# Moving the sum of squares of a gated norm from GpSimd alone to ScalarE and GpSimd, and reordering the work at a group's end

## The chip, the cores and the metric

One core of one Trainium2 chip runs the whole program. The metric is device time in microseconds (us) for one execution, the median of several runs. The engines are TensorE (PE in the profile, its weight loads PEld), VectorE (DVE), ScalarE (ACT), GpSimd (POOL) and SyncE (SP), which issues the DMAs. Each engine runs its own queue in order; the queues are tied together by semaphores alone.

## The reference, cut to what matters

The program is a chain of four blocks over 1024 tokens of 512 features (4 sequences of 256), each followed by `x = layernorm(x + block(x))`: A (a Taylor-like attention and a feed-forward), B (a feed-forward with LoRA), C (a Mamba2-like state space block) and D (a ternary feed-forward). The change touches C alone. Of it:

```
u      = x @ in_proj.T                 -> gate (8192), xs (8192), B, C (8 groups x 128), dt (128)
xs     = silu(causal_conv4(xs)),  B, C likewise
Y      = chunked scan(xs, dt, B, C) + xs * D                 (128 heads of 64)
y      = Y * silu(gate)
y      = y * rsqrt(mean of y*y over each group of 1024 + eps) * norm_w      (8 groups)
out    = y @ out_proj.T                                      (8192 -> 512)
```

The mean of squares runs over the 1024 features of a group, so the factor of a group is known only when all of the group's features are.

## The kernel before, in words

Stage C works on 64 units of 128 features (two heads of 64). Eight units make a group. Features stand on the partitions and the 1024 tokens along the free axis, in halves of 512, each in a PSUM bank. `Unit(g, p, j)` is unit `U = 8g + 2p + j`: group g, pair p (0 to 3), member j. `V = U - 1` is the unit before it. `for_units` writes the two bodies of pair 0 out and loops over pairs 1 to 3; group 0 is written out and groups 1 to 7 are a loop. After it comes a unit called `last`, which only finishes.

The units are software-pipelined by hand. The body of unit U does, on each engine, in this order:

* TensorE: input projection of x for U (`in_x`, 12 matmuls of 512 columns for each half), the scan's matmuls for V (`inside`), two small ones that make exponents (`seg`, L1712 and L1713), the gate's projection (`in_g`, 24 matmuls), four token tiles of the output projection of the pair before (`out_tile`, 6 matmuls each), and transposes (`turn`, L1746). All wide products are three fp32r products of split operands, a high part and a low part.
* VectorE: the last low part of y (`y_low`, L1210), the convolution (six L1124), `y_inside` (L1198) and `y_gated` (L1205) of V, `clamp` (eight L1242), and then the decay products (`decay_round`, six L1230, which count `m_done`) mixed with four `out_add` (L1221, which adds an output bank to `group_out`) and two `x_steps` (L1250).
* ScalarE: taps, the high part of the next x weights (L1468), SiLUs, exponentials (with two loads of its function table a unit, ahead of L1553 and L1539), the high part of the next gate weights (`gate_weights`, L1472), and high parts of y (`y_high`, L1505).
* GpSimd: the low parts of the weights (`low`, L1365, for x and for the gate; `out_low`, L1373) and the squares: `squares` waits until VectorE has done all six decay products of U, squares y of V (L1386) and adds the squares to `sq_sum` (L1389). For the first unit of a group L1384 writes the squares to `sq_sum` directly.

The order in GpSimd's body is: `out_low` (if j is 0), low part of the x weights, squares, low part of the gate weights, `out_low` (if j is 1), and the group's sums where a group has ended. TensorE's `in_g` waits for the gate's low part (`g_w_lo`), and `out_tile` of a j = 0 unit for `out_w_lo`.

A group's outputs are summed unscaled in `group_out` and scaled at the end. The last unit of a group is finished in the body of (g, 0, 0) of the next. In the body of (g, 0, 1) TensorE, after the first half of `in_x`, waits for the sum of squares and adds it over the partitions (`squares_sum`, 8 fp32 products with a vector of ones, L1757), VectorE takes the mean (`mean_square`), ScalarE the root, VectorE the reciprocal and the scaled addition of tiles 0 to 3 to x (`group_add`, L1271). ScalarE scales tiles 4 to 7 (`group_scaled`, L1572), GpSimd adds them to x (`group_sum`, L1396) and then clears the whole of `group_out` (L1399), all at the end of the same body. The next thing in GpSimd's queue is `out_low` of unit (g, 1, 0).

Of the kernel before, what the change touches and what calls it, by code (L numbers as in the profile page):

```python
# [10 lines left out]
ALU = mybir.AluOpType  # L11
# [5 lines left out]
P = 128  # L17
# [24 lines left out]
GROUPS = 8  # L42
# [860 lines left out]
class Unit:  # L903


    def __init__(self, g, p, j):
        self.g, self.p, self.j = g, p, j
        self.U = g * UPG + p * 2 + j
        self.V = self.U - 1
        self.first_pair = isinstance(g, int) and g == 0 and isinstance(p, int) and p == 0  # L910
        self.first = self.first_pair and j == 0
        self.group_first = isinstance(p, int) and p == 0 and j == 0
        self.after_group_first = isinstance(p, int) and p == 0 and j == 1
        self.group_ends = self.group_first and not self.first
        self.group_ended = self.after_group_first and not self.first_pair


def for_units(eng, body):

    def group(g):  # L920
        for j in range(2):
            body(Unit(g, 0, j))
        with eng.Fori(1, PAIRS) as p:
            for j in range(2):
                body(Unit(g, p, j))
    group(0)
    with eng.Fori(1, GROUPS) as g:
        group(g)


def state_space(nc, sh, dram):
# [3 lines left out]
    with Stage(nc) as ctx:  # L935
        def sb(name, shape, dt=F32):
            return ctx.enter_context(nc.sbuf_tensor(f"C_{name}", shape, dt))

        def sem(name):
# [34 lines left out]
        first_count = sb("first_count", [P, 2])  # L974
# [17 lines left out]
            group_zero""".split()  # L992
# [136 lines left out]
        def _(v):  # L1129
# [84 lines left out]
            def out_add(u, k):  # L1214

                t = 4 * u.j + k
                v.wait_ge(S.out_mm, (u.U - 2) * 4 + (k + 1))
                if k == 0:
                    v.wait_ge(S.out_added, (u.U - 2) * 4 + OUT0)
                    v.wait_ge(S.group_zero, u.g if u.group_first or u.after_group_first else u.g + 1)  # L1220
                v.tensor_tensor(group_out[:, t, :], bank[OUT_BANK[k % 4]][:, :], group_out[:, t, :], ALU.add)\  # L1221
                 .then_inc(S.out_added, 1)
# [38 lines left out]
            def group_scale(g):  # L1261
                v.wait_ge(S.std_done, g)
                v.wait_ge(S.group_done, (g - 1) * TT + ONE0)
                v.reciprocal(rstd[:, :], ms[:, :]).then_inc(S.rstd_done, 1)
# [17 lines left out]
            v.memset(first_count[:, 1:2], 0.0).then_inc(S.sq_added, ONE0)  # L1282
            v.wait_ge(S.consts_in, 32)
# [72 lines left out]
            for hf in range(2):  # L1356
                group_add(GROUPS, range(HT * hf, HT * (hf + 1)), (last.U - 2) * 4 + TT)
                v.wait_ge(S.group_done, (GROUPS - 1) * TT + HT * (hf + 1) + ONE0)
                norm.vector(v, hf)

        @block.gpsimd
        def _(e):
# [13 lines left out]
            def squares(u):  # L1376

                y, sq = xs[:, 1 - u.j, :], sg[:, 1 - u.j, :]
                e.wait_ge(S.gated, u.V * 2 + 2)
                if u is not last:  # L1380
                    e.wait_ge(S.m_done, u.U * ROUNDS + ROUNDS)
                if u.after_group_first:
                    wait(e, S.ms_mm, u.g)
                    e.tensor_tensor(sq_sum[:, :], y, y, ALU.mult).then_inc(S.squared, 1)  # L1384
                else:
                    e.tensor_tensor(sq, y, y, ALU.mult).then_inc(S.squared, 1)  # L1386
                    e.wait_ge(S.squared, u.U)
                    e.wait_ge(S.sq_added, added_before(u) + ONE0)
                    e.tensor_tensor(sq_sum[:, :], sq_sum[:, :], sq, ALU.add).then_inc(S.sq_added, 1)  # L1389

            def group_sum(u, g):

                for i in range(HT):
                    t = HT + i
                    e.wait_ge(S.group_scaled, (g - 1) * HT + (i + 1))
                    e.tensor_tensor(sh.x[:, t, :], group_out[:, t, :], sh.x[:, t, :], ALU.add).then_inc(S.group_done, 1)  # L1396
                e.wait_ge(S.group_zero, 1)
                e.wait_ge(S.group_done, g * TT + ONE0)
                e.memset(group_out[:, :, :], 0.0).then_inc(S.group_zero, 1)  # L1399
# [9 lines left out]
            e.wait_ge(S.dt_moved, 5)  # L1409
            e.wait_ge(S.dt_chain_v, DT_V)  # L1410
            e.memset(group_out[:, :, :], 0.0).then_inc(S.group_zero, 1)

            def body(u):
# [16 lines left out]
        def _(a):  # L1430
# [136 lines left out]

            def group_scaled(u, g):
                a.wait_ge(S.rstd_done, g + ONE0)
                a.wait_ge(S.out_added, (u.U - 1) * 4 + OUT0)  # L1570
# [4 lines left out]
            def body(u):  # L1575
# [25 lines left out]
            y_high(last, 0)  # L1601
            y_high(last, 1)
# [293 lines left out]
```

## Time and profile before

| what | value |
|---|---|
| median of 3 runs | 2421.09 us (2419.13 to 2422.48) |
| the profiled execution's own time | 2417.13 us |
| its span, first to last instruction | 2415.4 us |
| mean granted TensorE clock | 0.946 of full |
| TensorE busy in the span | 2165.9 us (90%) |
| VectorE, ScalarE, GpSimd busy | 1803.1, 1156.4, 826.7 us |

The span is the sum of four stages that run one after the other. Stage C begins at about 510 us, its units at about 650 us, and they end at about 2166 us. The share of an engine over the span says little about a stage: what matters is how long one unit takes, and what TensorE waits for in it.

### The profile page before, as it was taken

The numbers are of one execution on the slowest core, as the hardware profiler recorded it, in microseconds if no ns is written. First come the engines' busy times: TensorE is split into PE (matmuls) and PEld (weight loads), VectorE is DVE, ScalarE is ACT, GpSimd is POOL, SyncE is SP. The second block draws the span as 40 slices with busy tenths as digits, with TensorE's granted clock in tenths as the row PEclk, the third lists the DMA queues.
The fourth block names the chain that finished last, engine by engine and source line by source line (L and its number), as shares of the span: only waits on it lengthen the run. The fifth ranks groups of instructions, "written<-read, shape, count | busy, mean of one in ns | idle before, by whom it ended". The sixth has DMA issues, their size and how long they took to land. (4 is left out here: it accounts for less than half of the span.)

```text
span 2415.4 us, 36570 instructions
## 1 busy us (share of the span) xinstructions
PE 2165.9 (90%) x10769; PEld 1720.9 (71%) x10833; DVE 1803.1 (75%) x2969; ACT 1156.4 (48%) x2118; POOL 826.7 (34%) x478
## 2 busy tenths in 40 slices
PE   7999499979899989989989989989989989975987
PEld 6777387867777767767767777777777767754865
DVE  6444446449778878979878878878878878977887
ACT  2112114333366656655656656656656656631222
POOL 5434133411123434434344334425334443430000
PEclk9999699989999989989999999999999999987998
DMA  4211412322222212211221222211121221202433
GB/s 149 92 40 57 143 64 79 104 41 103 72 96 66 79 45 66 79 44 58 65 66 44 66 62 60 66 57 60 49 79 44 66 79 44 70 1 93 143 116 106
DMA packets 125941, 175.68 MB, mean 73 GB/s; under 512 B 17668, under 2 KB 83716, under 8 KB 125316
## 3 DMA queue, kind: packets, MB, share of 16 engines
q1 hardware_dynamic: 125892, 175.07, 22.8%
q8 instruction: 26, 0.43, 0.1%
q14 instruction: 23, 0.19, 0.0%
HBM read 165.72 MB, written 9.31 MB: 72 GB/s over the span
## 5 line engine op out<-in xcount | busy, mean ns | idle before, releaser
L70 PE MATMUL bank<-xT_hi,C_w_hi 128*128 128x512 f32 x1160 | 480.9, 415 | 32.1 <-POOL C_w_lo L1365 25.3
L71 PE MATMUL bank<-xT_lo,C_w_hi 128*128 128x512 f32 x1160 | 465.4, 401 | 0.0
L72 PE MATMUL bank<-xT_hi,C_w_lo 128*128 128x512 f32 x1160 | 465.3, 401 | 0.0
L1386 POOL TENSOR_TENSOR C_sg<-C_xs 128x1024 f32<-128x1024 f32 x56 | 130.8, 2336 | 677.3 <-DVE C_decay L1230 677.3
L1124 DVE SCALAR_TENSOR_TENSOR C_acc<-bank,C_par,C_acc 128x510 f32<-128x510 f32 (+2 forms) x384 | 285.8, 746 | 85.5 <-ACT C_acc L1432 56.3
L70 PEld LDWEIGHTS bank<-xT_hi,C_w_hi 128*128 128x128 f32 x1160 | 223.4, 193 | 97.8 <-POOL C_w_lo L1365 41.0
L72 PEld LDWEIGHTS bank<-xT_hi,C_w_lo 128*128 128x128 f32 x1160 | 222.4, 192 | 54.7
L1221 DVE TENSOR_TENSOR C_group_out<-bank,C_group_out 128x512 f32<-128x512 f32 x256 | 175.1, 687 | 112.4 <-PE bank L72 112.4
L71 PEld LDWEIGHTS bank<-xT_lo,C_w_hi 128*128 128x128 f32 x1160 | 223.6, 193 | 47.7
L1230 DVE TENSOR_TENSOR C_decay<-C_decay,C_cb 128x512 f32<-128x512 f32 x384 | 252.1, 685 | 3.9 <-ACT C_decay L1558 3.9
L1432 ACT ACTIVATE C_acc<-bank,C_par_two 128x512 f32<-128x512 f32 x128 | 98.8, 777 | 298.3 <-PE bank L72 291.3
L70 PE MATMUL bank<-C_out_hi,C_yg_hi 128*128 128x512 f32 x512 | 207.5, 405 | 32.8 <-POOL C_out_lo L1373 32.8
L1365 POOL TENSOR_TENSOR C_w_lo<-C_raw,C_w_hi 128x512 fp32r<-128x512 f32 x130 | 176.6, 1367 | 100.6 <-ACT C_w_hi L1468 89.7
L72 PE MATMUL bank<-C_out_hi,C_yg_lo 128*128 128x512 f32 x512 | 205.4, 401 | 0.0
L71 PE MATMUL bank<-C_out_lo,C_yg_hi 128*128 128x512 f32 x512 | 205.2, 401 | 0.0
L1505 ACT ACTIVATE C_yg_hi<-C_xs,C_par_two 128x512 fp32r<-128x512 f32 x128 | 92.6, 724 | 144.3 <-DVE C_xs L1205 94.4
L1692 PE MATMUL bank<-C_decay,C_xd 128*64 128x256 f32 x1024 | 158.6, 388 | 3.2 <-DVE C_decay L1230 3.2
L1553 ACT ACTIVATE C_decay<-C_cs_second,C_end_t 128x128 f32<-128x128 f32 x512 | 157.0, 389 | 0.8
L1205 DVE TENSOR_TENSOR C_xs<-C_xs,C_sg 128x512 f32<-128x512 f32 x128 | 147.2, 1150 | 4.4
L70 PEld LDWEIGHTS bank<-C_out_hi,C_yg_hi 128*128 128x128 f32 x512 | 100.0, 195 | 58.1 <-issue 30.9
L1389 POOL TENSOR_TENSOR C_sq_sum<-C_sq_sum,C_sg 128x1024 f32<-128x1024 f32 x56 | 133.2, 2378 | 6.9 <-POOL C_sg L1386 4.7
L1242 DVE TENSOR_SCALAR C_decay<-C_cs_second,C_cs_t 128x128 f32<-128x128 f32 x512 | 132.7, 357 | 2.6 <-DMA C_cs_second<-cs_rows 2.6
(245 smaller groups left out, 4457.9 us busy)
## 6 DMA issues: line engine op xcount, KB each, us to landing
C_raw<-in_Cxg SPq DMA_DIRECT2D x65, 512.0 KB, 3.5
C_cs_second<-cs_rows SPq DMA_DIRECT2D x64, 512.0 KB, 5.1
C_raw_out<-in_Cout SPq DMA_DIRECT2D x64, 256.0 KB, 3.7
D_raw<-in_D SPq DMA_DIRECT2D x32, 512.0 KB, 3.8
A_raw<-in_A SPq DMA_DIRECT2D x20, 512.0 KB, 3.6
B_right_raw<-in_D SPq DMA_DIRECT2D x16, 512.0 KB, 3.6
D_raw<-in_D SPq DMA_DIRECT2D x32, 256.0 KB, 2.6
cb_rows<-C_decay SPq DMA_DIRECT2D x8, 768.0 KB, 3.3
```

The costliest lines, as they stand in the source:

```text
L70: pe.matmul(out, lh, rh, start=start, stop=False)
L71: pe.matmul(out, lh, rl, start=False, stop=False)
L72: return pe.matmul(out, ll, rh, start=False, stop=stop)
L1124: v.scalar_tensor_tensor(out=sums[:, :, i:], in0=src[:, :].rearrange("p (b t) -> p b t", b=2)[:, :, 0:SEQ - i], scalar=w(TAPS - 1 - i), in ...
L1205: v.tensor_tensor(s, s, sg[:, 1 - u.j, half(h)], ALU.mult).then_inc(S.gated, 1)
L1221: v.tensor_tensor(group_out[:, t, :], bank[OUT_BANK[k % 4]][:, :], group_out[:, t, :], ALU.add)\
L1230: v.tensor_tensor(e, e, cb[:, r % 2 if r < 4 else 2, :], ALU.mult).then_inc(S.m_done, 1)
L1242: v.tensor_scalar(decay[:, 4 + h, t], cs_second[:, u.j, HALF * h + P * b:HALF * h + P * (b + 1)], cs_t[:, 2 * b + 1, bass.ds(u.U * 2 + h, ...
L1365: e.tensor_tensor(w_lo[:, slot, :], raw_at, f32(w_hi[:, slot, :]), ALU.subtract).then_inc(lo_done, 1)
L1389: e.tensor_tensor(sq_sum[:, :], sq_sum[:, :], sq, ALU.add).then_inc(S.sq_added, 1)
L1553: a.activation(decay[:, 2 * h + b // 2, SEQ * (b % 2) + CHUNK:SEQ * (b % 2 + 1)], cs_second[:, u.j, at:at + CHUNK], ACT.Exp, bias=end_t[:, ...
L1692: pe.matmul(bank[4 + th][q, at:at + SEQ], xd[:, 2 * b, q], decay[:, 2 * h + th, at:at + SEQ], start=True, stop=False)
```

## The change

1. The square of y moves from GpSimd to ScalarE (`square`, an ACTIVATE with the function Square on 128x1024), between `gate_weights` and the second `y_high`. It writes `sg`, or `sq_sum` for the first unit of a group. It no longer waits for VectorE's decay products.
2. GpSimd's `squares` is only the addition to `sq_sum`. It moves behind the low part of the gate weights, except in the body of (g, 0, 0), where it stays ahead of them and drops the wait for the decay products.
3. The scaling of tiles 4 to 7 on ScalarE and their addition on GpSimd move from the end of body (g, 0, 1) to the end of body (g, 1, 0).
4. `group_out` isn't cleared any more. In pair 1 of each group `out_add` is a copy of the bank, not an addition. The clear before the loop is gone too.
5. Pair 1 is written out like pair 0, and the loop runs over pairs 2 and 3.

```diff
@@ for_units
     def group(g):
-        for j in range(2):
-            body(Unit(g, 0, j))
-        with eng.Fori(1, PAIRS) as p:
+        for p in range(2):
+            for j in range(2):
+                body(Unit(g, p, j))
+        with eng.Fori(2, PAIRS) as p:
             for j in range(2):
                 body(Unit(g, p, j))
@@ vector: out_add
                 if k == 0:
                     v.wait_ge(S.out_added, (u.U - 2) * 4 + OUT0)
-                    v.wait_ge(S.group_zero, u.g if u.group_first or u.after_group_first else u.g + 1)
-                v.tensor_tensor(group_out[:, t, :], bank[OUT_BANK[k % 4]][:, :], group_out[:, t, :], ALU.add)\
-                 .then_inc(S.out_added, 1)
+                if not u.adds_first:
+                    v.tensor_tensor(group_out[:, t, :], bank[OUT_BANK[k % 4]][:, :], group_out[:, t, :], ALU.add)\
+                     .then_inc(S.out_added, 1)
+                    return
+                if k == 0:
...
+                    elif u.j == 0:
+                        v.wait_ge(S.group_done, u.g * HT + ONE0)
+                    else:
+                        v.wait_ge(S.group_summed, u.g * HT + ONE0)
+                v.tensor_copy(group_out[:, t, :], bank[OUT_BANK[k % 4]][:, :]).then_inc(S.out_added, 1)
@@ gpsimd
             def squares(u):
-                y, sq = xs[:, 1 - u.j, :], sg[:, 1 - u.j, :]
-                e.wait_ge(S.gated, u.V * 2 + 2)
-                if u is not last:
-                    e.wait_ge(S.m_done, u.U * ROUNDS + ROUNDS)
-                if u.after_group_first:
-                    wait(e, S.ms_mm, u.g)
-                    e.tensor_tensor(sq_sum[:, :], y, y, ALU.mult).then_inc(S.squared, 1)
-                else:
-                    e.tensor_tensor(sq, y, y, ALU.mult).then_inc(S.squared, 1)
+                if not u.after_group_first:
                     e.wait_ge(S.squared, u.U)
                     e.wait_ge(S.sq_added, added_before(u) + ONE0)
-                    e.tensor_tensor(sq_sum[:, :], sq_sum[:, :], sq, ALU.add).then_inc(S.sq_added, 1)
+                    if u is not last and not u.group_ends:
+                        e.wait_ge(S.m_done, u.U * ROUNDS + ROUNDS)
+                    e.tensor_tensor(sq_sum[:, :], sq_sum[:, :], sg[:, 1 - u.j, :], ALU.add).then_inc(S.sq_added, 1)
@@ group_sum
-                e.wait_ge(S.group_zero, 1)
-                e.wait_ge(S.group_done, g * TT + ONE0)
-                e.memset(group_out[:, :, :], 0.0).then_inc(S.group_zero, 1)
@@ body
                 low(S.x_w_hi, 0, raw[:, 1 - s, 0:D], S.x_w_lo, U + 2)
-                if not u.first:
+                if not u.first and u.group_ends:
                     squares(u)
                 low(S.g_w_hi, 1, raw[:, 1 - s, D:2 * D], S.g_w_lo, U + 2)
+                if not u.first and not u.group_ends:
+                    squares(u)
                 if u.j == 1:
                     out_low(u)
-                if u.group_ended:
+                if u.group_left:
                     group_sum(u, u.g)
@@ scalar
+            def square(u):
+                a.wait_ge(S.gated, u.V * 2 + 2)
+                if u.after_group_first:
+                    wait(a, S.ms_mm, u.g)
+                a.activation(sq_sum[:, :] if u.after_group_first else sg[:, 1 - u.j, :], xs[:, 1 - u.j, :], ACT.Square)\
+                 .then_inc(S.squared, 1)
...
                 gate_weights(u.U + 1, 1 - u.j)
                 if not u.first:
+                    square(u)
                     y_high(u, 1)
                 if u.j == 1:
                     out_weights(u)
-                if u.group_ended:
+                if u.group_left:
                     group_scaled(u, u.g)
```

Here `group_ends` is unit (g, 0, 0) with g over 0, `group_left` is (g, 1, 0) with g over 0, and `adds_first` is pair 1 of any group.

## Rows read from the trace of the kernel before

**Rows 1.** The page: busy time and share of each engine.

```profile
PE 2165.9 (90%) x10769; PEld 1720.9 (71%) x10833; DVE 1803.1 (75%) x2969; ACT 1156.4 (48%) x2118; POOL 826.7 (34%) x478
```

**Rows 2.** Timeline of PE: `seg`, a unit's mark (start, duration; first and last of 62 units).

```profile
702.04 0.19 PE L1713 MATMUL bank<-C_right_rest,C_left_rest 128*128 128x56 bf16 x1 [0.16 <-issue]
...
1018.87 0.19 PE L1713 MATMUL bank<-C_right_rest,C_left_rest 128*128 128x56 bf16 x1 [0.16 <-issue]
...
1051.54 0.19 PE L1713 MATMUL bank<-C_right_rest,C_left_rest 128*128 128x56 bf16 x1 [0.16 <-issue]
...
1072.50 0.19 PE L1713 MATMUL bank<-C_right_rest,C_left_rest 128*128 128x56 bf16 x1 [0.16 <-issue]
...
1099.24 0.19 PE L1713 MATMUL bank<-C_right_rest,C_left_rest 128*128 128x56 bf16 x1 [0.16 <-issue]
...
1120.83 0.19 PE L1713 MATMUL bank<-C_right_rest,C_left_rest 128*128 128x56 bf16 x1 [0.16 <-issue]
...
2126.97 0.19 PE L1713 MATMUL bank<-C_right_rest,C_left_rest 128*128 128x56 bf16 x1 [0.16 <-issue]
```

**Rows 3.** Timeline of PE: its waits inside units (bracket: idle time before, releaser).

```profile
1019.65 0.50 PE L70 MATMUL bank<-xT_hi,C_w_hi 128*128 128x512 f32 x1 [0.36 <-POOL C_w_lo L1365]
...
1040.05 3.57 PE L1757 MATMUL bank<-C_ones,C_sq_sum 128*128 128x1 f32 x16 [5.37 <-POOL C_sq_sum L1389]
...
1082.70 0.79 PE L70 MATMUL bank<-C_out_hi,C_yg_hi 128*128 128x512 f32 x1 [4.10 <-POOL C_out_lo L1373]
...
2153.09 0.80 PE L70 MATMUL bank<-C_out_hi,C_yg_hi 128*128 128x512 f32 x1 [5.36 <-POOL C_out_lo L1373]
```

**Rows 4.** Stretches: each engine's busy us, then PEclk, DMA share, GB/s.

```profile
1040.05:1043.60 3.55, 3.55 (x17) 3.55 (x17) 0.00 (x0) 0.00 (x0) 1.09 (x1) 0.50 0.31 89
1043.60:1048.60 5.00, 5.00 (x15) 3.68 (x14) 0.17 (x1) 0.00 (x0) 0.00 (x0) 0.55 0.62 199
...
1082.70:1089.60 6.90, 6.90 (x24) 5.62 (x25) 5.12 (x11) 4.97 (x8) 1.10 (x1) 0.78 0.00 0
...
2166.10:2168.00 1.90, 1.89 (x17) 1.77 (x16) 0.00 (x0) 0.00 (x0) 0.00 (x0) 1.00 0.00 0
```

**Rows 5.** Timeline of POOL: a group's end, the clear, and an ordinary unit.

```profile
1035.09 2.33 POOL L1386 TENSOR_TENSOR C_sg<-C_xs 128x1024 f32<-128x1024 f32 x1 [10.83 <-DVE C_decay L1230]
1037.58 2.34 POOL L1389 TENSOR_TENSOR C_sq_sum<-C_sq_sum,C_sg 128x1024 f32<-128x1024 f32 x1 [0.16 <-POOL C_sg L1386]
...
1077.79 3.52 POOL L1399 MEMSET C_group_out<- 128x4096 f32 x1
1081.26 1.30 POOL L1373 TENSOR_TENSOR C_out_lo<-C_raw_out,C_out_hi 128x512 fp32r<-128x512 f32 x1
...
1121.50 3.00 POOL L1373 TENSOR_TENSOR C_out_lo<-C_raw_out,C_out_hi 128x512 fp32r<-128x512 f32 x2
```

**Rows 6.** Timeline of DVE in an ordinary unit, and `clamp` under the clear.

```profile
1078.81 5.86 DVE L1242 TENSOR_SCALAR C_decay<-C_cs_second,C_cs_t 128x128 f32<-128x128 f32 x8
...
1121.77 1.58 DVE L1205 TENSOR_TENSOR C_xs<-C_xs,C_sg 128x512 f32<-128x512 f32 x1
...
1126.68 1.65 DVE L1242 TENSOR_SCALAR C_decay<-C_cs_second,C_cs_t 128x128 f32<-128x128 f32 x8
1129.06 0.69 DVE L1221 TENSOR_TENSOR C_group_out<-bank,C_group_out 128x512 f32<-128x512 f32 x1 [0.73 <-PE bank L72]
...
1132.67 1.28 DVE L1230 TENSOR_TENSOR C_decay<-C_decay,C_cb 128x512 f32<-128x512 f32 x2
```

**Rows 7.** Timeline of ACT: a 128x1024 activation, and an ordinary unit's end.

```profile
530.40 1.06 ACT L1453 ACTIVATE C_group_out<-C_group_out 128x1024 f32<-128x1024 f32 x1
...
1129.89 1.28 ACT L1539 ACT_TABLE_LOAD   x1
...
1132.16 0.63 ACT L1472 ACTIVATE C_w_hi<-C_raw 128x512 fp32r<-128x512 f32 x1
...
1136.74 0.78 ACT L1432 ACTIVATE C_acc<-bank,C_par_two 128x512 f32<-128x512 f32 x1 [3.00 <-PE bank L72]
```

More of the change, by code:

```diff
@@ L915, in __init__ @@
         self.group_ended = self.after_group_first and not self.first_pair
+        self.adds_first = isinstance(p, int) and p == 1
+        self.group_left = self.adds_first and j == 0 and not (isinstance(g, int) and g == 0)
 def for_units(eng, body):
     def group(g):
-        for j in range(2):
-            body(Unit(g, 0, j))
-        with eng.Fori(1, PAIRS) as p:
+        for p in range(2):
+            for j in range(2):
+                body(Unit(g, p, j))
+        with eng.Fori(2, PAIRS) as p:
             for j in range(2):
@@ L973, in state_space @@
         dt_bias, neg_a = dt_par[:, 0:1], dt_par[:, 1:2]
-        first_count = sb("first_count", [P, 2])
+        first_count = sb("first_count", [P, 3])
         ms = sb("ms", [P, TT])
@@ L991, in state_space @@
             squared sq_added ms_mm ms_done std_done rstd_done out_mm out_added group_scaled group_done
-            group_zero""".split()
+            group_summed""".split()
         S = type("S", (), {n: sem(n) for n in names})
@@ L1219, in out_add @@
                     v.wait_ge(S.out_added, (u.U - 2) * 4 + OUT0)
-                    v.wait_ge(S.group_zero, u.g if u.group_first or u.after_group_first else u.g + 1)
-                v.tensor_tensor(group_out[:, t, :], bank[OUT_BANK[k % 4]][:, :], group_out[:, t, :], ALU.add)\
-                 .then_inc(S.out_added, 1)
+                if not u.adds_first:
[3 more added lines that the diff above has]
+                if k == 0:
+                    if isinstance(u.g, int) and u.g == 0:
+                        v.wait_ge(S.dt_moved, 5)
+                        v.wait_ge(S.dt_chain_v, DT_V)
+                    elif u.j == 0:
[3 more added lines that the diff above has]
+                v.tensor_copy(group_out[:, t, :], bank[OUT_BANK[k % 4]][:, :]).then_inc(S.out_added, 1)
             def decay_round(u, r):
@@ L1262, in group_scale @@
                 v.wait_ge(S.std_done, g)
-                v.wait_ge(S.group_done, (g - 1) * TT + ONE0)
+                v.wait_ge(S.group_done, (g - 1) * HT + ONE0)
+                v.wait_ge(S.group_summed, (g - 1) * HT + ONE0)
                 v.reciprocal(rstd[:, :], ms[:, :]).then_inc(S.rstd_done, 1)
@@ L1282, in _ @@
             v.memset(first_count[:, 1:2], 0.0).then_inc(S.sq_added, ONE0)
+            v.memset(first_count[:, 2:3], 0.0).then_inc(S.group_summed, ONE0)
             v.wait_ge(S.consts_in, 32)
@@ L1357, in _ @@
                 group_add(GROUPS, range(HT * hf, HT * (hf + 1)), (last.U - 2) * 4 + TT)
-                v.wait_ge(S.group_done, (GROUPS - 1) * TT + HT * (hf + 1) + ONE0)
+                v.wait_ge(S.group_done, (GROUPS - 1) * HT + HT * (hf + 1) + ONE0)
                 norm.vector(v, hf)
@@ L1395, in group_sum @@
                     e.wait_ge(S.group_scaled, (g - 1) * HT + (i + 1))
-                    e.tensor_tensor(sh.x[:, t, :], group_out[:, t, :], sh.x[:, t, :], ALU.add).then_inc(S.group_done, 1)
-                e.wait_ge(S.group_zero, 1)
-                e.wait_ge(S.group_done, g * TT + ONE0)
-                e.memset(group_out[:, :, :], 0.0).then_inc(S.group_zero, 1)
+                    e.tensor_tensor(sh.x[:, t, :], group_out[:, t, :], sh.x[:, t, :], ALU.add).then_inc(S.group_summed, 1)
             e.wait_ge(S.dtw_hi, 1)
@@ L1408, in _ @@
             low(S.g_w_hi, 1, raw[:, 0, D:2 * D], S.g_w_lo, 1)
-            e.wait_ge(S.dt_moved, 5)
-            e.wait_ge(S.dt_chain_v, DT_V)
-            e.memset(group_out[:, :, :], 0.0).then_inc(S.group_zero, 1)
             def body(u):
@@ L1566, in root @@
                 a.activation(ms[:, :], ms[:, :], ACT.Sqrt).then_inc(S.std_done, 1)
+            def square(u):
[4 more added lines that the diff above has]
+                 .then_inc(S.squared, 1)
             def group_scaled(u, g):
                 a.wait_ge(S.rstd_done, g + ONE0)
-                a.wait_ge(S.out_added, (u.U - 1) * 4 + OUT0)
+                a.wait_ge(S.out_added, (u.U - 2) * 4 + OUT0)
                 for t in range(HT, TT):
@@ L1601, in _ @@
             y_high(last, 0)
+            square(last)
             y_high(last, 1)
```

## Prediction

> **What bounds the kernel now.** I read the page's engine line first. TensorE is busy for 90% of the span and VectorE for 75% [rows 1]; the reader should see that no engine is simply full, and that the answer lies inside stage C. So I looked at the units one by one, by the mark that each has on TensorE, its `seg` [rows 2]. From the first mark to the last there are 1424.93 us in 61 steps. Three lengths occur. An ordinary step is 21.59 us (1099.24 to 1120.83; its neighbours are alike). The step from (g, 0, 1) to (g, 1, 0) is 20.96 us. The two steps around it, where a group ends, are 32.67 us and 26.74 us.
>
> Then I asked what TensorE waits for in each [rows 3]. An ordinary unit has one wait, 0.36 us for the gate's low weights from GpSimd. The 20.96 us step has no such wait, so I take 20.96 us as TensorE's own length; the wait costs 21.59 - 20.96 = 0.6 us with the fill of its pipeline. In the 32.67 us step TensorE stands 5.37 us for the sum of squares. In the 26.74 us step it stands 4.10 us for the low part of the output weights. After `last` it stands 5.36 us for the same thing.
>
> The waits have a second price, and the stretches show it [rows 4]. After the 5.37 us wait the granted clock is 0.50, which is the level of 1.2 GHz, and the `squares_sum` matmuls take 3.57 us. In the tail, where TensorE comes to them straight from wide matmuls, the clock is 1.00 (2.4 GHz) and the same 16 fill about 1.9 us. The next 5 us run at 0.55, and the 6.9 us after the 4.10 us wait at 0.78.
>
> If nothing but TensorE's own length were left, 61 steps would take 61 x 20.96 = 1278.6 us. The excess is 146.4 us, and it splits as 7 x (32.67 - 20.96) = 82.0, 7 x (26.74 - 20.96) = 40.5, and 40 ordinary steps x 0.6 = 24. (61 less 14 at the group ends and 7 of 20.96 us leave 40.)
>
> **The change, part by part.**
>
> **The gate's low weights.** Before, they stood behind the square (2.33 us) and the addition (2.34 us), both of which wait for VectorE's last decay product [rows 5]. That closes a loop: decay products, squares, low weights, `in_g`, output tiles, `out_add`, decay products. Now the low part follows ScalarE's high part, which ends at 1132.79 [rows 7], some 8 us ahead of the next `in_g`. The loop is open, and the ordinary step goes to 20.96 us if VectorE and ScalarE can follow. Worth 24 us.
>
> **The square on ScalarE.** The nearest row is an activation on the same 128x1024 floats: 1.06 us [rows 7]. ScalarE idles 3.00 us a little later in the j = 0 body, before the next tap [rows 7], so the square hides there. In the j = 1 body the second `y_high` waits for the last `out_add` anyway. If its cover were gone it would cost 64 x 1.06 = 68 us. The bounds are nothing and that; I take nothing. No row shows Square itself. Its possible table load is a rival below.
>
> **The price on VectorE.** When VectorE multiplies two SBUF tensors while GpSimd works, it is held up: the L1205 at 1121.77 takes 1.58 us under GpSimd's `out_low` pair, against 0.64 us for a product of the same shape in a quiet place (two L1230 in 1.28 us) [rows 5, 6]. GpSimd suffers as well, 3.00 us for two that take 1.30 each. The low part now falls on the third and fourth decay products; the bounds are nothing and a full 1.28 us more per unit for VectorE. I take the full 1.2. Against that, GpSimd has 2.33 us less to do between the decay products and L1205, so it is nearly through by then, and the 0.9 us that L1205 loses today mostly comes back, about even. From `out_add` 0 to the last decay product VectorE has 12 instructions of 0.65, 7.8 us; with 1.2 it is 9.0. TensorE needs that last product only after three more tiles and two halves of `in_x`, 18 + 24 wide matmuls. 24 of them took 6.90 us at 0.78 of the clock [rows 4], so 0.224 us each at full clock and 9.4 us for 42, and the eight transposes between them add about 1 us. It fits by some 1.4 us. VectorE also still waits for TensorE at `out_add` (0.73 us, [rows 6]). So TensorE stays the bound.
>
> The Trainium skill ("SBUF — State Buffer", "SBUF: two separate sides") says that VectorE with two SBUF inputs and GpSimd take a shared port in turns, whoever comes first for the whole instruction. The trace agrees (1.58 us against 0.64 us). By that rule each GpSimd instruction moved in among the decay products would cost at most its own length once.
>
> **The group's end, sum of squares.** In body (g, 0, 0) ScalarE squares right after the gate weights, so in an ordinary unit's times at 1132.79 + 1.06 = 1133.9. GpSimd adds (2.34 us), perhaps after a decay product in progress: the sum is there between 1136.3 and 1136.9. TensorE ends the first half of `in_x` at about 1136.6 (the tap at 1136.74 follows it [rows 7]) less the 0.6 of the wait that is gone, 1136.0. So 5.37 us become 0.3 to 0.9; I take 0.9. The `squares_sum` matmuls then keep the high clock, 1.8 us instead of 3.57. For the clock after them I allow 0.6 of the roughly 2.2 us lost today. A group's end keeps 1.8 + 0.9 + 0.6 = 3.3 us over 20.96, in all 7 x 3.3 = 23 us. VectorE is blocked by the addition there for up to 2.4 us, but TensorE is itself 1.8 us later in that unit, so `inside` still finds its decay products.
>
> **The group's end, sums and clear.** The four additions and the clear (3.52 us) leave the queue ahead of `out_low` (1081.26 [rows 5]), whose result TensorE waits 4.10 us for. That wait goes whole, and so does the 5.86 us that `clamp` takes under the clear instead of 1.65 [rows 6]. What is late next: `group_sum` now begins after the addition of body (g, 1, 0), and four additions of 1.3 us put it 5.2 us into the next body. Behind it wait the low x weights, not needed until the following body, and the `out_add` of (g, 1, 1), which comes 4 us later. It may hold up an L1205 or two there, at most 1 to 2 us for VectorE, once a group, within the slack. ScalarE's four scalings (2.5 us) fall into its 3.00 us gap less 1.06: the tap may be 0.6 us late, behind VectorE's `y_low`. I price both at nothing; without cover they are 7 x 2.5 = 17 us. The copies in pair 1 read one input less and I price them like the additions, 0.69 us [rows 6], so at nothing. No DMA is added. The loads of weights wait for the low parts and can only start sooner.
>
> **The tail.** After `last`, `out_low` stands behind the squares and the gate's low part. Both are shorter or earlier; of 5.36 us I expect about 1.5 to stay (the low half of y is due then), with a little clock: 4.5 us gained.
>
> **Sum.** 146.4 - 23.1 + 4.5 = 127.8 us. The profiled execution took 2417.13 us, so 2289.3; the median of the runs is 4 us above it, so **2293 us**.
>
> **Rivals.**
>
> *VectorE becomes the bound of ordinary units* (17%). If the blocking costs more than my 1.4 us of slack, the ordinary step stays near 21.59 and only the group ends gain: 2293 + 24 = 2317. For it: 75% busy over the span is near 90% inside a unit. Against it: it still waits for TensorE in every unit.
>
> *The group's end keeps a wait and the low clock* (14%). If the addition comes 2 us later than I think, TensorE idles some 3 us, the clock falls again, `squares_sum` takes 3.57 and the next stretch is slow: 7 x (2.1 + 1.77 + 0.6) = 31, so 2324. For it: the 4.10 us wait alone was enough for a clock of 0.78 [rows 4]. Against it: the times above leave 0.9 us.
>
> *Square needs its own table* (5%). Then two loads of 1.28 us [rows 7] join each unit, 3.6 us with the square, about 1.9 us over what the j = 1 body can hide: up to 32 x 1.9 = 61, so 2354. Against it: the activation at 530.40 has no load before it, and copies run between the two tables.
>
> The Trainium skill ("ScalarE: Activation LUTs", "Table sets: the hidden batching unit") says that cheap functions such as copy and abs lie in every set; it does not name square among them.
>
> *Slower* (3%). If every instruction that GpSimd now runs near the decay products (1.28 + 2.34) stopped VectorE for its whole length, with no relief at L1205, and TensorE waited for all of it, a unit would be 21.5 - 1.2 + 3.6 = 23.9 us. That is 61 x 2.3 = 140 us lost against 104 gained at the group ends and the tail: 2457. It decides from 1.7 us more per unit. Against it: the decay products wait for GpSimd's addition nowhere but in body (g, 0, 0).
>
> *Nothing of note* (1%): the waits are all replaced by equals, 2420.
>
> **How the numbers follow.** The forecast's own case has 60%, from 2281 (no residual wait, no clock loss) to 2305. The two likeliest rivals end at 2317 and 2324, so the range goes from 2281 to 2330 and leaves out the table, the slower case and both rivals at once. A measurement tells 0.2%, about 5 us. Faster 0.95, same 0.01, slower 0.04.
>
> **What would show it.** Marks 20.96 to 21.1 us apart in ordinary units; around 24.3 us for the step over `squares_sum`, whose matmuls take 1.84 us; no wait of TensorE for the low part of the output weights but in the tail; no idle for the gate's low weights; one Square of about 1.06 us per unit with no new table load; decay products stretched to about 1.9 us once a unit; the mean clock above 0.96. I am wrong if TensorE waits for decay products or convolutions in ordinary units, or if a table load stands before Square.

## The result, and the profile after

The changed kernel takes 2313.47 us (2312.29 to 2314.32, 4 runs) against 2421.11 us before: a ratio of 0.9556, with a 95% interval of 0.9539 to 0.9572. That is 107.6 us less. The forecast was 2293 us, 127.8 us less, with a range from 2281 to 2330.

The page of the changed kernel, its engine line (compare [rows 1]) and the decay products:

```profile
PE 2132.7 (92%) x10769; PEld 1700.1 (74%) x10833; DVE 1762.6 (76%) x2970; ACT 1214.7 (53%) x2182; POOL 673.3 (29%) x406
...
L1243 DVE TENSOR_TENSOR C_decay<-C_decay,C_cb 128x512 f32<-128x512 f32 x384 | 299.1, 807 | 4.5 <-ACT C_decay L1563 4.5
```

GpSimd has lost 153 us of work and ScalarE gained 58. The decay products (L1243 now) take 807 ns on average, where the kernel before has 685 ns (L1230).

The marks of the units on TensorE, from its timeline (compare [rows 2]; the first, two ordinary steps, a group's end and what follows, the last of 62):

```profile
702.05 0.19 PE L1727 MATMUL bank<-C_right_rest,C_left_rest 128*128 128x56 bf16 x1 [0.16 <-issue]
...
979.55 0.19 PE L1727 MATMUL bank<-C_right_rest,C_left_rest 128*128 128x56 bf16 x1 [0.16 <-issue]
...
1000.53 0.19 PE L1727 MATMUL bank<-C_right_rest,C_left_rest 128*128 128x56 bf16 x1 [0.16 <-issue]
...
1027.81 0.19 PE L1727 MATMUL bank<-C_right_rest,C_left_rest 128*128 128x56 bf16 x1 [0.16 <-issue]
...
1048.77 0.19 PE L1727 MATMUL bank<-C_right_rest,C_left_rest 128*128 128x56 bf16 x1 [0.16 <-issue]
...
1069.75 0.19 PE L1727 MATMUL bank<-C_right_rest,C_left_rest 128*128 128x56 bf16 x1 [0.16 <-issue]
...
2023.41 0.19 PE L1727 MATMUL bank<-C_right_rest,C_left_rest 128*128 128x56 bf16 x1 [0.16 <-issue]
```

An ordinary step is 1000.53 - 979.55 = 20.98 us, and so is the one that held the 4.10 us wait (1048.77 to 1069.75). All 61 steps take 1321.4 us, 103.6 less than before, and the profiled execution as a whole 104.9 less (a span of 2310.5 us against 2415.4). Only the step over `squares_sum` is off the forecast: 27.28 us here, not 24.3. The seven are 25.48, 27.28, 27.00, 27.27, 27.06, 27.29 and 26.50 us. They average 26.84. The first one is the shortest, and that is the clue.

What stands in that step, from the timeline: TensorE's two waits, then ScalarE, VectorE and GpSimd in the same stretch.

```profile
1007.75 0.49 PE L70 MATMUL bank<-C_out_hi,C_yg_hi 128*128 128x512 f32 x1 [1.11 <-DVE C_yg_lo L1213]
1018.51 1.94 PE L1771 MATMUL bank<-C_ones,C_sq_sum 128*128 128x1 f32 x16 [1.35 <-POOL C_sq_sum L1398]
...
997.87 0.63 ACT L1484 ACTIVATE C_out_hi<-C_raw_out 128x512 fp32r<-128x512 f32 x1 [2.64 <-issue]
1014.79 1.06 ACT L1577 ACTIVATE C_sg<-C_xs 128x1024 f32<-128x1024 f32 x1
...
999.33 0.75 DVE L1127 SCALAR_TENSOR_TENSOR C_acc<-bank,C_par,C_acc 128x510 f32<-128x510 f32 x1 [2.42 <-ACT C_acc L1437]
...
1016.01 2.37 POOL L1398 TENSOR_TENSOR C_sq_sum<-C_sq_sum,C_sg 128x1024 f32<-128x1024 f32 x1 [13.12 <-ACT C_sg L1577]
```

Compare [rows 3]: of 5.37 us for the sum of squares 1.35 stay, and a wait of 1.11 us for the low half of y is new. It goes back to ScalarE, which stands 2.64 us with nothing named that it waits for ("issue"). Its row is the first instruction behind the jump back of the loop over groups. So VectorE's convolution begins 2.42 us late, then y. It happens at the start of groups 2 to 7 (2.32 to 2.65 us), not of group 1, which the program enters without a jump.

The stretches from there on (columns as in [rows 4]):

```profile
1018.50:1020.50 2.00, 1.99 (x17) 2.00 (x18) 2.00 (x2) 0.00 (x0) 1.55 (x1) 1.00 0.00 0
1020.50:1025.00 4.50, 4.50 (x14) 3.28 (x15) 2.33 (x5) 0.06 (x1) 0.00 (x0) 0.62 0.70 233
```

The narrow matmuls run at full clock and take 1.94 us instead of 3.57. But behind them the granted clock falls to 0.62 for some 4.5 us, in all seven groups.

### The profile page after: what moved, and what is told of

Same layout as the page of the kernel before. It is cut to its first block and busy times, and to the rows that moved or that the text cites. A ratio compares the mean times of both kernels' runs of the same rounds, so it can differ in the third digit from the quotient of the medians.

```text
span 2310.5 us, 36141 instructions
## 1 busy us (share of the span) xinstructions
PE 2132.7 (92%) x10769; PEld 1700.1 (74%) x10833; DVE 1762.6 (76%) x2970; ACT 1214.7 (53%) x2182; POOL 673.3 (29%) x406
## 5 line engine op out<-in xcount | busy, mean ns | idle before, releaser
L1380 POOL TENSOR_TENSOR C_w_lo<-C_raw,C_w_hi 128x512 fp32r<-128x512 f32 x130 | 186.7, 1436 | 736.5 <-ACT C_w_hi L1477 640.3
L1243 DVE TENSOR_TENSOR C_decay<-C_decay,C_cb 128x512 f32<-128x512 f32 x384 | 299.1, 807 | 4.5 <-ACT C_decay L1563 4.5
L1398 POOL TENSOR_TENSOR C_sq_sum<-C_sq_sum,C_sg 128x1024 f32<-128x1024 f32 x56 | 154.3, 2756 | 212.8 <-DVE C_decay L1243 121.5
L70 PE MATMUL bank<-C_out_hi,C_yg_hi 128*128 128x512 f32 x512 | 202.0, 395 | 7.8 <-DVE C_yg_lo L1213 5.5
L71 PE MATMUL bank<-C_out_lo,C_yg_hi 128*128 128x512 f32 x512 | 200.0, 391 | 0.0
L1224 DVE TENSOR_TENSOR C_group_out<-bank,C_group_out 128x512 f32<-128x512 f32 x192 | 131.0, 687 | 81.9 <-PE bank L72 81.9
L1537 ACT ACTIVATE C_xs<-C_acc 128x512 f32<-128x512 f32 x128 | 80.5, 629 | 140.6 <-DVE C_acc L1127 140.5
L1213 DVE SCALAR_TENSOR_TENSOR C_yg_lo<-C_xs,C_par,C_yg_hi 128x512 fp32r<-128x512 f32 x128 | 113.3, 885 | 3.5 <-ACT C_yg_hi L1510 3.4
L72 PEld LDWEIGHTS bank<-C_out_hi,C_yg_lo 128*128 128x128 f32 x512 | 96.5, 189 | 21.3
```

The costliest lines, as they stand in the source:

```text
L70: pe.matmul(out, lh, rh, start=start, stop=False)
L71: pe.matmul(out, lh, rl, start=False, stop=False)
L72: return pe.matmul(out, ll, rh, start=False, stop=stop)
L1213: v.scalar_tensor_tensor(out=yg_lo[:, slot, half(h)], in0=xs[:, slot, half(h)], scalar=par_of(V, NORM_W), in1=f32(yg_hi[:, slot, half(h)]) ...
L1243: v.tensor_tensor(e, e, cb[:, r % 2 if r < 4 else 2, :], ALU.mult).then_inc(S.m_done, 1)
L1380: e.tensor_tensor(w_lo[:, slot, :], raw_at, f32(w_hi[:, slot, :]), ALU.subtract).then_inc(lo_done, 1)
```

## The experiments

Medians of 4 runs each (10 for the run that only writes pair 1 out); the kernel before, run beside them, took 2419.7 to 2421.8 us. The steps are those of the profiled execution. Group 1 is entered without a jump, groups 2 to 7 by one.

| run | us | step over squares_sum, groups 1 to 7 |
|---|---|---|
| changed kernel | 2313.5 | 25.5, 27.3, 27.0, 27.3, 27.1, 27.3, 26.5 |
| e1_act_flat | 2295.9 | 25.5, 25.5, then five of 24.0 |
| e2_low_behind | 2304.5 | 23.6, 26.1, 26.0, 24.5, 26.0, 27.6, 24.7 |
| e3_pool_squares | 2322.3 | 24.7, 28.0, 28.0, 26.4, 26.4, 28.0, 26.4 |
| e4_only_unrolled | 2421.0 | 32.5, 32.4, 31.9, 33.1, 32.7, 32.5, 32.4 |
| e5_flat_behind | 2305.4 | 23.6, 26.0, 24.6, 27.6, 27.6, 26.1, 24.5 |
| e6_early_square | 2311.4 | 25.3, 24.7, 27.0, 24.7, 27.0, 24.7, 27.0 |
| e7_pool_all_behind | 2342.6 | 25.3, then 27.1 six times |
| e8_two_squares | 2347.9 | 27.4, 31.5, 30.3, 31.4, 31.4, 29.7, 31.3 |
| e9_sums_back | 2314.9 | 25.5, 26.6, 26.5, 27.3, 28.7, 27.0, 27.1 |
| e10_end_as_others | 2341.2 | 30.9, 31.9, 32.7, 31.8, 30.6, 32.4, 31.7 |
| e11_all_flat | 2307.2 | 25.4, 23.7, 25.4, then 27.0 four times |
| e12_sum_later | 2301.0 | 25.6, 26.7, 24.0, 24.0, 25.7, 24.0, 24.0 |

**ScalarE's group loop written out** (changed kernel otherwise; ScalarE alone calls `for_units` with `flat=True`).

```diff
     group(0)
+    if flat:
+        for g in range(1, GROUPS):
+            group(g)
+        return
     with eng.Fori(1, GROUPS) as g:
```

> The changed kernel with ScalarE's loop over groups 1 to 7 written out (its inner loop over pairs 2 and 3 stays); the other engines as they are. Theory F (the 2.3 to 2.6 us for which ScalarE stands at the start of a group, where the profile names nothing that it waits for, come from its jump back over six written bodies): the stall is gone, TensorE no longer waits about 1.1 us for the low half of y in body (g, 0, 0), and the step over squares_sum goes from 27.2 us to the 25.5 us that group 1 has, which is entered without a jump. 6 x 1.7 = 10 us, so 2303 us. Rival G (the stall is one of code that was not lately run, jump or no jump): it shows up at other places of the written-out code, seven times or more, and the time is 2313 us or above.

2295.94 us, ratio to the kernel before 0.9485 (0.9469 to 0.9501): 17.5 us less than the changed kernel. The stall is gone, and so is TensorE's wait for y in body (g, 0, 0). Every wait for the sum is 0.90 us, as in group 1 before. So theory F holds, but the gain is larger than the 10 us that it gave. The steps say why: in five groups of seven the clock does not fall. Timeline of PE and two stretches of this run, group 2 and group 3 (the last but two number of a stretch is the granted clock):

```profile
1017.45 1.94 PE L1775 MATMUL bank<-C_ones,C_sq_sum 128*128 128x1 f32 x16 [0.90 <-POOL C_sq_sum L1402]
1190.52 1.94 PE L1775 MATMUL bank<-C_ones,C_sq_sum 128*128 128x1 f32 x16 [0.90 <-POOL C_sq_sum L1402]
```

```profile
1019.40:1024.00 4.60, 4.60 (x16) 3.09 (x18) 2.36 (x5) 0.47 (x1) 0.00 (x0) 0.65 0.73 232
...
1192.40:1197.00 4.60, 4.60 (x33) 3.54 (x34) 3.18 (x6) 1.59 (x3) 0.21 (x1) 1.00 0.75 227
```

The same pause and the same matmuls, and once 0.65, once 1.00. Five steps are 1.5 us shorter for it, 7.5 us; the stall and its two waits account for the other 6 x 1.6 = 9.5 us. Why the clock held in five groups here and in none of the changed kernel isn't shown.

**The 2 x 2 of square and order.** The changed kernel has the squares on ScalarE and the gate's low weights ahead of the addition. The other three corners:

```diff
e2_low_behind:
-                if not u.first and u.group_ends:
+                if not u.first:
                     squares(u)
                 low(S.g_w_hi, 1, raw[:, 1 - s, D:2 * D], S.g_w_lo, U + 2)
-                if not u.first and not u.group_ends:
-                    squares(u)
e3_pool_squares (gpsimd, and no square() on ScalarE):
...
+                e.wait_ge(S.gated, u.V * 2 + 2)
+                if u is not last and not u.group_ends:
+                    e.wait_ge(S.m_done, u.U * ROUNDS + ROUNDS)
+                if u.after_group_first:
+                    wait(e, S.ms_mm, u.g)
+                    e.tensor_tensor(sq_sum[:, :], y, y, ALU.mult).then_inc(S.squared, 1)
+                else:
+                    e.tensor_tensor(sq, y, y, ALU.mult).then_inc(S.squared, 1)
...
e7_pool_all_behind: both
```

> The changed kernel with the gate's low weights behind GpSimd's addition again in every unit. Theory A (the ordinary step fell to 20.98 us because the square left GpSimd's queue, the order being a second safeguard): the low weights come 2.8 + 1.3 us after the last decay product, just ahead of the gate's projection, so steps stay at 20.98 and the time within 3 us of 2313. Rival B (the new order is what opened the loop): TensorE waits again 0.2 to 0.4 us for the low weights in ordinary units, step 21.2 to 21.5, 40 x 0.2 to 0.5 = 10 to 20 us more, 2323 to 2333.

> The changed kernel with the squares taken by GpSimd again, at the new places: reordered group ends alone. Theory C (the order does it all; ScalarE's squares bring nothing, and at a group's end they come late, behind ScalarE's exponentials): ordinary steps 20.98, and since GpSimd can square right after y is gated, the sum of squares is done 4 us earlier at a group's end, TensorE's wait of 0.9 to 1.35 us for it goes, 7 x 1.2 = 8 us off: 2305. Rival D (4.7 us of GpSimd work behind the last decay product hold up VectorE's gating and the low weights of x): steps of 21.1 to 21.5, 2320 to 2335.

> The changed kernel with the squares on GpSimd again and the gate's low weights behind them, as before the change; only the group ends are reordered. Theory A (GpSimd's square and addition ahead of the gate's low weights close the loop through TensorE and VectorE): ordinary steps are back at 21.5 to 21.6 us, so 40 x 0.6 = 24 us over the changed kernel less what the reordered group ends give, about 2325 to 2345. Rival B' (the ordinary steps fell for another reason, the missing clear or the unrolled pair): they stay near 20.98.

| | low weights behind | low weights ahead |
|---|---|---|
| squares on GpSimd | 2342.6, steps 21.5 to 21.6 | 2322.3, steps 20.98, but two a group |
| squares on ScalarE | 2304.5, steps 20.98 | 2313.5, steps 20.98 |

With neither, ordinary steps are back at 21.50 to 21.60 us and TensorE again waits 0.34 to 0.46 us for the gate's low weights in most units (once a group 1.1 to 1.2 us, in a step of 22.3). Either edit alone opens the loop. So theory A holds for the steps, and the order was no necessity. Its time was missed (within 3 us of 2313): with the square gone from GpSimd, the old order is 9 us better. There the low weights no longer run among VectorE's decay products, and TensorE has no wait for y in groups 2 to 7, although ScalarE stalls as before (2.35 to 2.61 us). Those six waits were 5.4 us of the 9; the rest lies in how far the clock fell, and no run shows that this comes from the order.

Theory C fails. With GpSimd squaring, TensorE indeed never waits for the sum, but it then waits at `inside`, and one ordinary step a group is 22.1 us and one 21.4. The wait for the low half of y is still there (1.08 to 1.11 us). Rival D's time came (2320 to 2335), but not its longer step in every unit. Timeline of PE in that run:

```profile
1025.67 1.12 PE L1710 MATMUL bank<-C_decay,C_xd 128*64 128x256 f32 x4 [2.23 <-issue]
```

The wait in front of L1710 has no releaser in the row; in the program it is for the decay products.

**Pair 1 written out, in the kernel before.**

```diff
-        for j in range(2):
-            body(Unit(g, 0, j))
-        with eng.Fori(1, PAIRS) as p:
+        for p in range(2):
+            for j in range(2):
+                body(Unit(g, p, j))
+        with eng.Fori(2, PAIRS) as p:
```

> The kernel before with pair 1 written out and nothing else: the same work in the same order, more code in the loop over groups. Theory F: ScalarE stands 2.3 to 2.6 us at the start of groups 2 to 7 here too, and since no wait for low weights can hide it all, the time rises by 0 to 1.1 x 6 = 7 us over 2421. Rival G': the stall belongs to something else in the change and does not appear; 2421 as before.

2421.02 us, ratio 0.9997 (0.9987 to 1.0006). The stall is there, in ScalarE's timeline at each start of groups 2 to 7 (2.30 to 2.52 us), where the kernel before has 0.15. Timelines of ScalarE, VectorE and TensorE:

```profile
1014.86 0.63 ACT L1480 ACTIVATE C_out_hi<-C_raw_out 128x512 fp32r<-128x512 f32 x1 [2.39 <-issue]
...
1024.17 0.74 DVE L1211 SCALAR_TENSOR_TENSOR C_yg_lo<-C_xs,C_par,C_yg_hi 128x512 fp32r<-128x512 f32 x1
...
1025.24 0.42 PE L70 MATMUL bank<-C_out_hi,C_yg_hi 128*128 128x512 f32 x1
```

It costs nothing there: the low half of y is done at 1024.91, and TensorE comes to the output tiles at 1025.24, without a wait. That is 27.96 us after the group's last mark (997.28). In the changed kernel TensorE is there after 27.1 us (1007.75 - 1.11 - 979.55), ahead of the low half of y, which is done after 27.95. So what hid the stall was the loop through the gate's low weights: it made TensorE late in the unit before and again in this one. It was not the 5.37 us wait for the sum, for e7_pool_all_behind has the loop and the stall (2.32 to 2.51 us) and no wait for the sum, and TensorE comes to the output tiles at 27.94 to 27.98 us and waits for no y either. In e3_pool_squares, which differs from it in the order alone and has the loop open, TensorE is there at 27.1 us and waits 1.08 to 1.11 us for y. The change opened the loop, and with it took the cover away.

**Every Square twice**, with a wait between (priced work, no other output).

```diff
+                a.activation(..., xs[:, 1 - u.j, :], ACT.Square).then_inc(S.squared_once, 1)
+                a.wait_ge(S.squared_once, u.U)
                 a.activation(..., xs[:, 1 - u.j, :], ACT.Square).then_inc(S.squared, 1)
```

> The changed kernel with every Square done twice, with a wait between the two, to price the cover of the first on ScalarE. Theory L (in ordinary units the square lies in ScalarE's idle time, at a group's end it does not): ordinary steps stay at 20.98, the wait for the sum of squares grows by 1.2 to 1.3 us, 7 x 1.25 = 9 us and up to 3 more by the clock, 2322 to 2326 us. Rival M (ScalarE is nearly the bound): ordinary steps grow by 0.3 to 1.1 us, 2335 to 2380 us.

2347.86 us, 34.4 more than with one. Most ordinary steps stay at 20.98, but one a group is 21.3 to 21.7, one 22.1 and one 21.2: some 1.7 us a group. The time lies in rival M's range, but not by its road. The rest is at the group's end, and its size was in neither theory: ScalarE's stall doubles.

```profile
1006.18 0.63 ACT L1484 ACTIVATE C_out_hi<-C_raw_out 128x512 fp32r<-128x512 f32 x1 [4.90 <-issue]
```

It is 4.5 to 4.9 us in five of six groups, with one activation and one wait more in each body. TensorE then waits 3.77 to 4.17 us for the low half of y. So the stall grew when code was added between the jump and its target; but the sixth, over the same code, is 2.61 us, so the length of the code alone doesn't set it.

**The group's end.** Three runs, each on the changed kernel or on e1_act_flat.

```diff
e10_end_as_others (GpSimd's addition in (g, 0, 0) as in other bodies):
-                    if u is not last and not u.group_ends:
+                    if u is not last:
...
-                if not u.first and u.group_ends:
-                    squares(u)
                 low(S.g_w_hi, 1, raw[:, 1 - s, D:2 * D], S.g_w_lo, U + 2)
-                if not u.first and not u.group_ends:
+                if not u.first:
                     squares(u)
e9_sums_back (scaling and sums of tiles 4 to 7, both engines):
-                a.wait_ge(S.out_added, (u.U - 2) * 4 + OUT0)
+                a.wait_ge(S.out_added, (u.U - 1) * 4 + OUT0)
...
-                if u.group_left:
+                if u.group_ended:
e12_sum_later (on e1_act_flat):
                 in_x(u, 0)
+                in_x(u, 1)
                 if u.group_ended:
                     squares_sum(u)
-                in_x(u, 1)
```

> The changed kernel with GpSimd's addition in body (g, 0, 0) where it is in all other bodies: behind the gate's low weights and waiting for the last decay product. Prices that special case. From the trace: the addition would begin about 2 us later and take 2.4 to 2.8 us, so TensorE waits 2.5 to 3.5 us instead of 0.9 to 1.35, its clock falls ahead of the narrow matmuls (3.57 us instead of 1.94) in some groups: 7 x 2 to 5 us, 2328 to 2348 us. Rival: VectorE's decay products are free of the addition, y comes sooner, and half of it is given back: 2318 to 2325.

2341.22 us, 27.7 more: this special case is worth that. TensorE waits 3.32 to 4.43 us for the sum, longer than expected, and the narrow matmuls are back at 3.57 us in all seven groups.

> The changed kernel with ScalarE's scaling of tiles 4 to 7 and GpSimd's addition of them back at the end of body (g, 0, 1); the clear stays out and the squares stay on ScalarE. Theory N (the move matters: four additions of 1.3 us ahead of out_low keep TensorE waiting in (g, 1, 0), since there they begin about 5 us ahead of where the clear began before, and take 5.2 us): a wait of 0.5 to 1.5 us and a lower clock behind it, 7 x 1 to 3, 2320 to 2335 us. Rival O (taking the clear out was enough): no such wait, 2313 us or less, since the overrun of the sums into body (g, 1, 1) is gone too.

2314.86 us, 1.4 more than the changed kernel, which is within the noise. Rival O holds. TensorE has no wait for the low part of the output weights, though the four sums stand in front of it (5.96 us, in the timeline of GpSimd):

```profile
1044.29 5.96 POOL L1405 TENSOR_TENSOR x_tokens<-C_group_out,x_tokens 128x512 f32<-128x512 f32 x4
1050.21 1.27 POOL L1388 TENSOR_TENSOR C_out_lo<-C_raw_out,C_out_hi 128x512 fp32r<-128x512 f32 x1
```

So the 4.10 us wait had ended with what left the queue, the clear of 3.52 us and the square of 2.34 us before it; moving the sums a body on brought nothing more in time. In e3_pool_squares and e7_pool_all_behind GpSimd squares, and the clear and the sums have left its queue; the wait is gone there too, so the square alone did not keep it. (The clear alone wasn't tried.) The second step after each group's end is 0.3 to 0.45 us longer with the sums at the old place.

> The run with ScalarE's group loop written out, with squares_sum behind both halves of in_x instead of between them. The sum of squares is long there (0.9 us late before, 2.8 us of matmuls moved ahead of it), so TensorE comes to the narrow matmuls without a pause. Theory Q (the pause and the narrow matmuls together lower the clock in some groups): the clock stays at 1.00 in all seven, the step is 20.98 + 1.94 + at most 0.5, 23.0 to 23.4 us, so 7 x 0.7 + 2 x 1.5 = 8 us off 2296, 2288. Rival R (the narrow matmuls alone lower it): steps of 24.5 to 25.0 us in some or all groups, 2292 to 2300. Rival S (inside now waits for VectorE's mean_square): steps of 24 us and more at full clock, 2296 or above.

2301.03 us, 5 more than e1_act_flat. The wait for the sum is gone and a wait of 1.27 us at `inside` has come, with ordinary steps of 21.1 to 21.7 once a group. Rival S holds. And the clock still falls behind the narrow matmuls in three groups, though no pause stands ahead of them there.

**Both gains together, and two more tries.**

> The two edits that gained, together: ScalarE's group loop written out, and the gate's low weights behind GpSimd's addition in every unit. Theory H (the two gains are one: both make the low half of y at a group's end come early enough, one by taking ScalarE's stall away, the other by keeping GpSimd off VectorE's decay products): TensorE still waits 0.9 us for the sum of squares, steps of 23.96 us where the clock holds, and the time is that of the first alone, 2296 within 4 us. Rival I (they add up, 17.5 + 9 us): 2287 us.

2305.40 us: they do not add up, the two together are worse than e1_act_flat alone by 9.5 us. Neither H nor I gave that. The clock falls in four groups, twice by more, and three times a step of 22.6 us comes up in pair 2. There VectorE and GpSimd meet (timelines of this run):

```profile
911.83 2.98 DVE L1217 SCALAR_TENSOR_TENSOR C_yg_lo<-C_xs,C_par,C_yg_hi 128x512 fp32r<-128x512 f32 x1
911.87 2.39 POOL L1402 TENSOR_TENSOR C_sq_sum<-C_sq_sum,C_sg 128x1024 f32<-128x1024 f32 x1 [11.77 <-DVE C_decay L1247]
```

A `y_low` that takes 0.74 us elsewhere lasts 2.98 us, until the addition of 2.39 us is over. It happens in the three groups with a step of 22.6 us and in no other, and in the next unit TensorE waits 1.35 to 1.40 us for the low half of y.

The Trainium skill ("SBUF — State Buffer", "SBUF: two separate sides") says that whichever of the two starts first has the shared port for its whole instruction, and that the other is blocked. The length agrees with that. The order of the starts doesn't: by the trace `y_low` began 0.04 us ahead of the addition that it waited for.

```diff
e6_early_square (on e5_flat_behind):
                 decay_exp(u)
+                if u.group_ends:
+                    square(u)
                 gate_silu(u, 0)
...
-                    square(u)
+                    if not u.group_ends:
+                        square(u)
```

> As the run with both edits, and in body (g, 0, 0) ScalarE squares ahead of the gate's SiLU, 2.8 us sooner. Theory J (the 0.9 us for which TensorE waits for the sum of squares is ScalarE's lateness, and the clock falls in some groups only because of that pause with the narrow matmuls behind it): the wait is gone, every step over squares_sum is 23.0 us with the clock at full, 7 x 0.9 plus up to 2 x 1.5 = 6 to 9 us less than the run beside it. Rival K (the addition now stops VectorE's decay products sooner, and inside waits for them instead): the wait only changes its name and the time stays within 3 us, or rises.

2311.37 us, 6 more than the run beside it. There is no wait for the sum, but 1.72 to 2.45 us at `inside` instead: rival K.

The next run writes out the loops of all engines (`flat=True` for each):

> The run with ScalarE's group loop written out, and the loops over groups of TensorE, VectorE, GpSimd and SyncE written out too. Theory F: only ScalarE's jump had a price, since no other engine shows time without a cause at a group's start: 2296 within 3 us. Rival P (TensorE's code is the longest, and code read once only comes too slowly): pauses without a cause on TensorE, 2300 to 2330 us.

2307.21 us, 11.3 more than with ScalarE's alone. Theory F's time was missed; rival P's came, but not its pauses. Ordinary steps are 20.98 (one a group 21.3, in five groups) and TensorE's waits are no longer than in e1_act_flat, 0.82 us for the sum, with one of 0.62 us at `inside`. The group ends carry the difference: their seven steps sum to 182.3 us against 170.8, and the clock falls already in the narrow matmuls, which take 2.38 to 2.57 us in groups 4 to 7.

The premise that no other engine stands without a cause at a group's start is not quite true. In e2_low_behind, e4_only_unrolled, e5_flat_behind, e6_early_square and e7_pool_all_behind VectorE too stands 0.43 to 0.90 us ahead of its first instruction there, at each start of groups 2 to 7. No run shows that this costs anything.

## Why the prediction came out as it did

Its main line held: the time lies in the range, 20 us above the forecast. In the profiled execution the gain is 104.9 us of 127.8, so 23 us are missing. (The medians show less missing because the kernel before was profiled 4 us under its median and the changed kernel only 1.2.) Term by term, from the traces of the changed kernel:

* *The loop through the low weights, 24 us.* Right: the 54 steps outside `squares_sum` take 20.99 us on average, 0.03 over the forecast's 20.96, together 1.6 us. The experiments show that one half of the change would have done it.
* *The wait of 4.10 us in (g, 1, 0), 40.5 us.* Right: the step is 20.98. It was the work that left the queue altogether that ended it; the move of the sums to the next body was not needed for it.
* *The square is hidden on ScalarE.* Right for one Square. The cover is short: a second one costs. Square takes 1.06 us, and no table load was added (157 in either kernel, none ahead of a Square). That rival is out.
* *VectorE pays up to 1.2 us for the low weights and gets as much back.* Roughly so. The decay products take 6 x 0.12 = 0.7 us more in a unit, and L1208, two a unit, 0.80 us instead of the 1.15 of L1205 before. TensorE stayed the bound, and the rival in which VectorE takes over in ordinary units did not come.
* *The group's end, 3.3 us over an ordinary step.* Too small: 5.86 on average. This is where the missing time is, 7 x 2.6 = 18 us.
  - "I allow 0.6 for the clock" is the first term that was too small. In group 1, where nothing else went amiss, the wait was 0.90 us as forecast and the narrow matmuls took 1.94 (1.8 in the sum), but the step is 4.5 us over. With the same wait and the clock held it is 3.0 us over in e1_act_flat. So the lower clock behind them cost 1.5 us, in all seven groups, and wait and matmuls 0.3 us more than the 2.7 allowed: 7 x 1.2 = 8.5 us too little.
  - The second is a step that the prediction lacks. It listed pair 1 written out as an edit and gave it no price. That code makes ScalarE stand 2.3 to 2.65 us at each start of groups 2 to 7. Behind it come the convolution, y and the square. TensorE pays up to 1.1 us at the output tiles and 0.45 us more at the sum, together with what follows 6 x 1.6 = 9.5 us. e1_act_flat takes the stall and these waits away, and e4_only_unrolled brings the stall into the kernel before, where it is free.
* *The tail, 4.5 us.* Only 1.3 (from the last mark to the end 288.4 us before, 287.1 after). The wait of 5.36 us at the output tiles became one of 2.29, not 1.5. But the wait for the decay products, which the prediction did not price, went from 3.19 to 4.26 us, and the clock behind it from 0.62 to 0.53.

The rival in which the group's end keeps a wait and a low clock had 14%. Of it only the low clock behind the narrow matmuls came; its wait of some 3 us and its narrow matmuls of 3.57 us did not. Three of the signs that the prediction named missed: the step over `squares_sum` (26.8 us, not 24.3), its matmuls (1.94 us, not 1.84) and the mean clock (0.958, not above 0.96).

What stays open is what decides whether the clock falls behind the narrow matmuls. With one and the same wait of 0.90 us the step is 24.0 or 25.5 us in e1_act_flat, and with one of 0.82 us it is 25.4 or 27.0 in e11_all_flat. A later place for the sum did not keep it up, a pause did not always bring it down, and kernels that differ only in other engines' loops differ in it by 11 us. So of the gains of single runs here up to some 10 us are of that kind, and 9 us between e2_low_behind and the changed kernel are not all the order's.

## What to carry to other kernels

When a wait is removed, ask what it was hiding: here a stall of 2.4 us cost nothing while TensorE came to the output tiles 0.9 us later, and 9.5 us in all once it came on time. Only running the layout of the code alone showed it. When two edits aim at one loop, run each alone; the second may cost more than it adds, and here the best version (2295.9 us) came from taking a jump away and not from more reordering. When work is moved in among another engine's, price it with the whole length of the longest instruction that it can meet, as the 2.98 us `y_low` shows.

## What the runs showed of the hardware

* ScalarE stood still at its jump back over written-out code: 0.15 us over four bodies (two of them an inner loop's) in the kernel before, 2.3 to 2.65 us over six, and 4.5 to 4.9 us, once 2.61, with one more activation and wait in each body. Without the jump (e1_act_flat) the stall is gone. The page of the changed kernel counts 93 packets on one of the two instruction queues, where the kernel before has 23; but the kernel with the doubled stall has 93 as well, and e1_act_flat without a stall has 75. That the stall is the fetching of code fits the jump and its absence in straight code; no run shows it directly.
* After 0.9 us of pause and 1.94 us of one-column matmuls the granted clock fell to about 0.65 for 4.6 us in one group and stayed at 1.00 in five others of the same run (e1_act_flat).
